# Decay exponents in a gated delta-rule layer: from a TensorE product to broadcast row sums with a per-partition bias

## Time and profile before

| | us |
|---|---|
| median of 3 runs | 4610.79 (4610.07 to 4611.10) |
| span of the profiled execution | 4601.9 |
| the median less that span | 8.9 |

### The profile page before, as it was taken

The page is one execution under the profiler, slowest core; times in us unless marked ns, Lnnn a source line. Parts: engine busy times, 40 slices in busy tenths (PEclk is TensorE's granted clock), DMA queues, the critical chain, the costliest instruction groups (busy, mean ns, idle before and its releaser), DMA issues. The chain is left out here.

```text
span 4601.9 us, 94001 instructions
## 1 busy us (share of the span) xinstructions
PE 4346.1 (94%) x31188; PEld 3239.7 (70%) x31188; DVE 3834.6 (83%) x8326; ACT 2846.0 (62%) x5356; POOL 2695.4 (59%) x8592
## 2 busy tenths in 40 slices
PE   4799999999999999999999999999999999998798
PEld 2477777777777777777777777777777777776444
DVE  6688988889888898888988889888888888985554
ACT  3466666666666666666666666666666666664111
POOL 1566666666666666666666666666666666664000
PEclk7899999999999999999999999999999999999899
DMA  3212212122121221212121221222222122120200
GB/s 106 45 41 48 49 35 48 41 48 50 34 59 39 50 48 34 50 48 50 36 58 42 47 48 39 45 50 48 48 47 46 42 47 49 38 44 20 70 14 19
DMA packets 575837, 209.77 MB, mean 46 GB/s; under 512 B 455180, under 2 KB 539660, under 8 KB 574328
## 3 DMA queue, kind: packets, MB, share of 16 engines
q1 hardware_dynamic: 574392, 200.48, 19.4%
q0 software_dynamic: 960, 3.28, 0.3%
HBM read 155.84 MB, written 47.81 MB: 44 GB/s over the span
## 5 line engine op out<-in xcount | busy, mean ns | idle before, releaser
L740 DVE SCALAR_TENSOR_TENSOR CV<-pp,CW,CV 128x1023 f32<-128x1023 f32 (+2 forms) x768 | 980.5, 1277 | 41.4 <-ACT CV L1122 24.5
L343 PE MATMUL pp<-A,W 128*128 128x512 f32 x2048 | 963.7, 599 | 14.9 <-DVE CV L740 9.3
L1414 POOL TENSOR_TENSOR UL<-UL,TM 128x126 f32<-128x126 f32 (+22 forms) x1984 | 735.1, 370 | 155.4
L1411 POOL TENSOR_TENSOR TM<-UL,XL 128x126 f32<-128x126 f32 (+22 forms) x1984 | 706.4, 356 | 148.3 <-issue 13.6
L343 PEld LDWEIGHTS pp<-A,W 128*128 128x128 f32 x2048 | 373.5, 193 | 312.8 <-issue 293.3
L1210 ACT ACTIVATE QE<-qa,TAB 128x128 f32<-128x128 f32 x1024 | 318.3, 362 | 425.6 <-PE qa L482 425.5
L863 DVE SCALAR_TENSOR_TENSOR St<-St,TAB,kv 128x128 f32<-128x128 f32 x1024 | 308.7, 343 | 234.9 <-PE kv L501 227.1
L1221 ACT ACTIVATE VS<-qa,EB 128x128 f32<-128x128 f32 x1024 | 319.2, 364 | 292.0 <-PE qa L492 286.0
L545 PE MATMUL emit<-Wo,NTr 128*128 128x256 f32 x2048 | 487.5, 381 | 1.1 <-ACT NTr L1255 1.1
L524 PE MATMUL emit<-Wz,A 128*128 128x256 f32 x2048 | 484.9, 380 | 1.6 <-DVE A L914 1.6
L900 DVE SCALAR_TENSOR_TENSOR CO<-CO,ty,SZ 128x128 f32<-128x128 f32 x1024 | 420.4, 469 | 64.3 <-POOL ty L1398 60.6
(11 more groups left out here) (232 smaller groups left out, 9463.4 us busy)
## 6 DMA issues: line engine op xcount, KB each, us to landing
W<-wqkv SPq DMA_DIRECT2D x256, 128.0 KB, 3.7
XL<-xb SPq DMA_DIRECT2D x128, 256.0 KB, 4.1
UL<-c_u SPq DMA_DIRECT2D x64, 256.0 KB, 2.9
xb<-X SPq DMA_DIRECT2D x512, 32.0 KB, 1.6
Wz<-wz SPq DMA_DIRECT2D x64, 256.0 KB, 2.7
ub<-UL SPq DMA_DIRECT2D x128, 128.0 KB, 2.9
N<-ub SPq DMA_DIRECT2D x256, 64.0 KB, 2.2
Wo<-wo SPq DMA_DIRECT2D x64, 256.0 KB, 3.8
```

The lines of the kernel that those rows point to most:

```text
L343: ins = t.matmul(bk.pp[:, 512 * h:512 * h + 512], m.W[:, c, k, :], m.xnT[:, w // KH % 2, c, 512 * h:512 * h + 512], start=c == 0, stop=c == 1)
L740: v.scalar_tensor_tensor(m.CV[:, t, d:S], bk.pp[:, 0:S - d], m.CW[:, w % KH, t, 3 - d:4 - d], m.CV[:, t, d:S], ALU.mult, ALU.add).then_inc ...
L1411: gp.tensor_tensor(m.TM[:, 0:a, 0:b], m.UL[:, 0:a, k:k + 1].to_broadcast([128, a, b]), m.XL[:, k, k + 1:32].unsqueeze(1).to_broadcast([128 ...
L1414: gp.tensor_tensor(m.UL[:, 0:a, k + 1:32], m.UL[:, 0:a, k + 1:32], m.TM[:, 0:a, 0:b], ALU.subtract).then_inc(s["sub"], 1)
```

## The change

Row sums stay in f32. The first one (gc, as rows) is written whole to DRAM, and one transfer per unit broadcasts the unit's two rows of 1024 values to all 128 partitions of a new tile GB (1 MB per unit, two buffers). The mask (0 or -1e30) is added to GB: on GpSimd (`gm`, two instructions of 128 x 1024 per unit), for units 0 and 1 on VectorE (`gmd`). The second row sum, as columns (AB), is the per-partition bias of the exponential: `dec` is now four ACTIVATEs of 128 x 128 for each quarter, sixteen per unit, in place in GB. `decp` and `mk` are gone, with GL, GR, DEC and the bf16 pieces. All four `dec` of a unit stand in ACT's order on both sides of `qe` of chunk 3, before `sz`. Each of `x` and `att` reads GB in place of DEC.

```diff
 SP
     def ldg(w):
-        sp.wait_ge(s["decp"], 4 * w)
-        for r in range(2):
-            q.dma_start(m.GR[3 * r:3 * r + 3, r, :], dr.gcd[2 * kh + r, :, t0:t0 + S]).then_inc(s["dg"], 16)
-        q.dma_start(m.GL[6:12], dr.gad[2 * kh:2 * kh + 2, :, t0:t0 + S]...).then_inc(s["dg"], 16)
+        sp.wait_ge(s["g3a"], 16)
+        if w > 1:
+            sp.wait_ge(s["strip"], STRIP["kq", w - 2, 3] + 1)
+        q.dma_start(m.GB[w % 2][:].rearrange("p r c t -> p r (c t)"),
+                    dr.gcd[32 * b + 2 * kh:32 * b + 2 * kh + 2, :].unsqueeze(0).to_broadcast([128, 2, S])).then_inc(s["dg"], 16)
+        if w:
+            sp.wait_ge(s["tabw"], 80)
+            sp.wait_ge(s["dec"], 4 * (w - 1))
+            q.dma_start(m.AB[w % 2][:], dr.abd[kh, :, b * CH:(b + 1) * CH, :]).then_inc(s["dg"], 16)
 start:
-        for k, d in enumerate((dr.gcd, dr.gad)):
-            sp.wait_ge(s["pieces"], 5 * k + 5)
-            q.dma_start(d[:, :, 0:S], p.pieces[k][0:32]).then_inc(s["g3a"], 16)
+        sp.wait_ge(s["gst"], 5)
+        q.dma_start(dr.gcd, p.ra).then_inc(s["g3a"], 16)
+        ldg(0)
 before the loop:
         xl(0)
+        ldg(1)
         ldw(1, 2)
 loop:
             decoded(u + 1)
-            ldg(u + 2)
+            ldg(u + 3)
             uo(u + 1)
 PE loop: the four decp(u + 2, q) are gone; pj(0, 2, h) moves from before the barrier to behind it
             qs(u, 5)
-            decp(u + 2, 0)
             pj(u + 2, 2, 0)
...
             sup(u, 5)
-            decp(u + 2, 1)
             at(u, 5)
...
             pj(u + 2, 2, 1)
-            decp(u + 2, 2)
             vn(u, 6)
...
             z(u, 2)
-            decp(u + 2, 3)
             m1(u + 1)
 DVE
-        v.tensor_tensor(m.DEC[n % 2][:], by(bk.strip[:], 4), g.mask..., ALU.min).then_inc(s["strip"], 1)
+    def gmd(w, r):
+        dv.wait_ge(s["dg"], 16 + 32 * w)
+        v.tensor_tensor(m.GB[w % 2][:, r], m.GB[w % 2][:, r], g.mask..., ALU.add).then_inc(s["gmd"], 1)
 DVE start: the ten instructions that make the pieces are gone; kred(0) moves behind the barrier
 DVE tables:
         dv.wait_ge(s["col"], 4)
+        v.tensor_copy(m.AB[0][:], p.BT[:, 0:CH, 0:2]).then_inc(s["ab"], 1)
+        for r in range(2):
+            gmd(0, r)
+        v.tensor_copy(tab(p, ROWJ), cols(p.BT)).then_inc(s["dtab"], 1)
 DVE loop: mk(u + 1, 0) to mk(u + 1, 3) are gone; gmd(1, 0) and gmd(1, 1) stand before the loop
 ACT
     def dec(w, q):
-        ac.wait_ge(s["strip"], STRIP["dec", w, q] + 1)
-        a.activation(m.DEC[n % 2][:], m.DEC[n % 2][:], ACT.Exp).then_inc(s["dec"], 1)
+        if w < 2:
+            ac.wait_ge(s["gmd"], 2 * w + 2)
+        else:
+            ac.wait_ge(s["gm"], 2 * (w - 1))
+        for c in range(2):
+            for r in range(2):
+                row = m.GB[w % 2][:, r, 2 * q + c, :]
+                ins = a.activation(row, row, ACT.Exp, bias=m.AB[w % 2][:, 2 * q + c, r:r + 1])
+        ins.then_inc(s["dec"], 1)
 ACT tables: dec(0, 0) to dec(0, 3) stand before the exponential of EGLB
 ACT loop:
             vs(u - 1, 2)
             vne(u - 1, 2)
+            dec(u + 1, 0)
+            dec(u + 1, 1)
             qe(u - 1, 3)
+            dec(u + 1, 2)
+            dec(u + 1, 3)
             sz(u - 1, 0)
             qt(u + 1)
             vs(u - 1, 3)
...
             qe(u - 1, 5)
-            dec(u + 1, 0)
             vs(u - 1, 5)
...
             sz(u - 1, 1)
-            dec(u + 1, 1)
             qe(u - 1, 6)
...
             vne(u - 1, 6)
-            dec(u + 1, 2)
             sz(u - 1, 2)
...
             nt(u - 1, 2)
-            dec(u + 1, 3)
             sq(u - 1, 3)
 POOL
+    def gm(w, r):
+        po.wait_ge(s["dg"], 16 + 32 * w)
+        gp.tensor_tensor(m.GB[w % 2][:, r], m.GB[w % 2][:, r], g.mask..., ALU.add).then_inc(s["gm"], 1)
 POOL start: the six gp.dma_start of the pieces are gone, nk(0) moves behind the barrier; tables writes a fifth table (abd)
 POOL loop:
             vsc(u + 1, 0)
+            gm(u + 3, 0)
+            gm(u + 3, 1)
             tv(u, 2)
```

More of the change, by code:

```diff
@@ L28 @@
 MAGIC = 1597463007.0
-EG, NEG, EGLB, EGLS = range(4)
+EG, NEG, EGLB, EGLS, ROWJ = range(5)
 SUB = 62
@@ L297, in loop @@
         nl(0)
+        ldg(2)
         ui(1)
@@ L374, in tpq @@
         ins.then_inc(s["tpq"], 1)
[L376 to L384, removed]
     def kq(w, q):
@@ L606, in loop @@
         tables()
-        decp(0, 0)
+        pj(0, 2, 0)
+        pj(0, 2, 1)
         kq(0, 0)
-        decp(0, 1)
         kq(0, 1)
-        decp(0, 2)
         kq(0, 2)
-        decp(0, 3)
         kq(0, 3)
@@ L1309, in tables @@
                          ACT.Exp).then_inc(s["egt"], 1)
+        for i in range(4):
+            dec(0, i)
         a.activation(tab(p, EGLB), cols(p.DL), ACT.Exp).then_inc(s["egt"], 1)
@@ L1431, in ng @@
                         ALU.mult).then_inc(s["EB"], 1)
+    def gm(w, r):
+        if not inside(w):
+            return
+        po.wait_ge(s["dg"], 16 + 32 * w)
+        gp.tensor_tensor(m.GB[w % 2][:, r], m.GB[w % 2][:, r], g.mask.unsqueeze(1).to_broadcast([128, CH, 128]),
+                        ALU.add).then_inc(s["gm"], 1)
     def vsc(w, h):
@@ L1477, in start @@
         gp.memset(m.N1[1][:], 0.0)
-        nk(0)
-        for k, d in enumerate((dr.gcd, dr.gad)):
-            po.wait_ge(s["pieces"], 5 * k + 5)
-            for b in range(1, NB):
-                gp.dma_start(d[:, :, b * S:b * S + S], p.pieces[k][32 * b:32 * b + 32]).then_inc(s["g3w"], 16)
     def tables():
         po.wait_ge(s["egt"], 4)
-        po.wait_ge(s["dtab"], 1)
+        po.wait_ge(s["dtab"], 2)
         for k in range(4):
@@ L1802, in program @@
 def program(nc, x, wqkv, wz, wo, convw, wba, dtb, alog, normw, lut, widx,
-            c_f32, c_mask, c_gr, c_reset, c_u0, out):
+            c_f32, c_mask, c_reset, c_u0, out):
     with ExitStack() as ctx:
@@ L1848, in program @@
             m.V = [alloc(lp, f"V{i}", [128, CH, 2, 128]) for i in range(2)]
-            m.DEC = [alloc(lp, f"DEC{i}", [128, 4, 128]) for i in range(2)]
+            m.GB = [alloc(lp, f"GB{i}", [128, 2, CH, 128]) for i in range(2)]
+            m.AB = [alloc(lp, f"AB{i}", [128, CH, 2]) for i in range(2)]
             m.X = [alloc(lp, f"X{i}", [128, 2 * CH, 128]) for i in range(2)]
@@ L1887, in program @@
             p.ra, p.rb, p.rc, p.rd = (m.QK[:, i, :] for i in (1, 2, 4, 5))
-            p.pieces = [m.X[1][:].rearrange("p u d -> p (u d)"), m.V[1][:].rearrange("p c r d -> p (c r d)")]
-            p.pieces = [t[:, 0:1536].bitcast(BF16).rearrange("p (k t) -> p k t", k=3) for t in p.pieces]
             p.GC, p.BT = (m.K[i][:].rearrange("p c (t h) -> p (c t) h", h=32) for i in (1, 2))
@@ L1940, in consts @@
     f[:, 128] = 1.0
[L1941 to L1943 removed]
+    mask = np.where(j > q, -1e30, 0.0).astype(np.float32)
     u0 = np.zeros((2, 64, 16, 32), np.float32)
```

129 lines of the change are left out of this document (42 added, 87 removed), and 2 rows, old and new, of the table SEMS.

## The result

The changed kernel takes 5080.62 us (median of 4 runs, 5065.87 to 5095.99); the kernel before 4610.94 in the same session (4610.07 to 4615.53). The ratio is 1.1024, 95% interval 1.1007 to 1.1041: 10% slower, where 0.6% was forecast. The range ended at 4725, so the result lies outside it.

The account below looks back on a forecast made before the run. PE was taken to set the pace; stall 1.92 less gain 1.27 gave +0.65 a turn, +40 us over 62 turns, less 12 at the start, plus 8.9 carried to the timed median: 4639 us, range 4565 to 4725.

Parts of the forecast that it names:

- What bounds the kernel: Steady turn of 64.03 us: PE, busy 62.55, sets the pace; other engines' delays cost only once PE must wait.
- What is hidden: POOL's two mask adds, 3.75 us together with 1.89 each, fit its idle 3.69 us before tv 2.
- if that cover were gone: If POOL's idle time did not cover the adds, nrm 2 on DVE would be late by the rest.
- The stall at `sup` 3: ACT's block of table loads and exponentials (0.26 us each) makes PE wait 1.92 us a turn at sup 3.
- still covered: DVE's state 3 starts near 2134.3 instead of 2134.1, before PE reaches ks 4 near 2135.2: no wait.
- Rival C: The stall at sup 3 lowers the granted clock, 1.4 us of slowness a turn: 4726 us; chance 0.06.
- The forecast without holds: Whole kernel with the adds hidden and the exponentials in one block: a turn of 64.7 us, 4639 us.
- PE's gain of 1.27: Second half of the turn: without decp and mk, PE gains 1.27 us a turn, bounds 0.9 and 1.9.
- Start: Work before the barrier goes, PE starts 16 us earlier; after costs, net 12 us gained, bounds 3 and 20.
- rival B: ACT's exponentials don't overlap, 0.362 us each: stall 3.5, net +2.25 a turn, 4738 us; chance 0.09.
- rival A: ACT's block (under about 4.8 us) is hidden, only PE's shorter list counts: 4520 us; chance 0.08.

Follow-up runs that it names:

- gm_dve: The changed kernel with the mask adds of all units on VectorE in front of nrm 0, none on GpSimd, exponentials still in one block; 4764.26 us.
- early_two_vsc_late: Changed kernel, mask adds on VectorE behind nrm 3, exponentials in two blocks (behind vne 2 and sz 1), GpSimd's first vsc moved behind nk; 4543.94 us.
- before_vsc_late: The kernel before, with only GpSimd's first vsc moved from behind on 1 to behind nk, in front of the second vsc; 4565.02 us.
- both: The changed kernel with GpSimd's mask adds issued after the second vsc and the exponentials in four groups at the old places; 4684.27 us.

## Why the prediction was wrong

- **What bounds the kernel.** Right: PE sets the pace, and a delay elsewhere costs one for one from the moment at which PE asks.
- **"What is hidden: the adds only take `vsc`'s place as `nrm` 1's neighbour."** This step failed, and with it 6.1 of the 7.1 us a turn that were missed (4.41 at `ctp` 1 and 1.66 behind it). I read the 1.96 of the earlier trace rows as a mild slowing and asked only whether POOL had 3.75 us free. It nearly had (3.69); the adds took 4.73, one 2.39 and not the 1.89 of `vsc`, which is not the same form (it takes one value per row where the adds take the mask), and that 1 us is in the hold too. The earlier trace rows held more: 0.83 us over the free 1.13 is one instruction of 1.17 us, which began when `vsc` had 1.02 to go and ended 0.15 behind it. Beside three GpSimd instructions in a row each of the first three is held. A cover of idle time on the engine that gets the work says nothing about the engine next to it. The prediction's words for "if that cover were gone" named `nrm` 2, the wrong victim.
- **The stall at `sup` 3.** Predicted 1.92, measured 2.34. The mechanism was right; the term mis-sized was the exponential: 0.26 taken from `qe`, 0.295 measured (eight in 2.36 us to the next start). The Trainium skill's figure (ScalarE: Activation LUTs, What ACT_TABLE_LOAD costs), an estimate of 0.29 us and a stall of 2.4, agrees with the trace. Its drain of 1.38 us doesn't show, and here the measurement decides: the exponentials begin 1.29 after the load does, and that is the load's own 1.28.
- **`state` behind the block "still covered".** Right: `ks` 4 starts directly behind `ctp` 0 at 2063.16, without a wait. But PE now waits for St 0.5 us a turn at `ks` 6, where the trace of before has nearly nothing. `decp` 1 and the 0.17 us that it waited for `att` stood in front of that `ks`; without them PE asks 0.39 us sooner, and `state` 5 starts 0.19 later behind its `sup` than before (0.83 for 0.64 us). So part of what the shorter list gives is lost there.
- **Rival C.** The slow clock came, behind the 5 us wait. The stall at `sup` 3 alone can do the same. In gm_dve, with that stall in every turn and no hold by adds, the way from `sup` 3 to the next `vn` takes 5.3 to 5.4 us in 28 turns and 6.8 to 7.0 in 32; in the changed kernel it is slow in 2 of 58. Two such stretches of gm_dve, in the order of the earlier trace rows (the clock is the third number from the end):

```profile
2145.07:2150.42 5.35, 5.34 (x34) 4.88 (x35) 5.32 (x11) 4.04 (x8) 4.51 (x11) 1.00 0.00 0
2211.32:2218.31 6.99, 6.99 (x34) 6.34 (x35) 6.80 (x12) 4.14 (x8) 5.37 (x15) 0.76 0.01 2
```

  That is 0.9 us a turn (32 of 60 turns at 1.65), so C, at 0.06, was a part of the truth for the kernel with the adds hidden. What decides which turns are slow stays open.
- **The forecast without holds.** gm_dve measured 4764 for 4639. Of the 125 us, 18.6 lie at the start, as told above. Its turn is 66.3 us, where 64.7 was forecast: 1.6 a turn. The terms that I find are 0.42 at `sup` 3, 0.54 at `ks` and 0.9 of slow matmuls, 1.9 in all; against them stands a wait of `decp` for `att` that went with it (13.7 us in all before), 0.2 a turn. Even with the failed step mended I should have been 2.6% low, from the same habit of taking each cover as whole.
- **PE's gain of 1.27.** In the steady turns it hardly reaches the end. early_two_vsc_late and before_vsc_late have the same turn within 0.05 us, though PE's list is 1.1 us shorter in the first; 0.6 of the 1.27 was `mk` 1 in front of `ctp` 1, and that wait is gone in both. The wait for St takes back about half of the 1.1 (36.2 us in all). How the rest divides between ScalarE's four table loads and the adds on VectorE (2.35 us) was not measured.
- **Start.** Predicted `x` of quarter 3 at 105.5; measured 106.65 (119.10 before). PE's first transposes behind the barrier start at 64.44, near 67 predicted, and `pj` waits for W once, 4.4 us. The state is first cleared at 169.6 us, 9.4 earlier than before, for a net 12 predicted. The steps held. The broadcast landed in 4.9 us where 7.7 was taken, and no wait of GpSimd between 300 and 4500 us names a transfer.
- **Two slips of arithmetic.** The net of rival B is 3.5 - 1.27 = 2.23 a turn, not 2.25, and rival A's block of 4.8 us needs exponentials of 0.14 (4.8 less two loads, over 16), not 0.12. Neither moves the forecast.

## What to carry to other kernels

Idle time on GpSimd isn't free to fill: list what VectorE executes beside it, and if that has two operands in SBUF, or is a lookup of the `lm` kind, price it at the full length of the longest GpSimd instruction. A row of four instructions whose mean is 1.7 times that of its equals elsewhere is a hold that is already there, and moving its neighbour may be the cheapest gain in the kernel (here 0.9% by one line). When two costs share a place, take both away before judging either. And before a difference of two times is divided by the number of turns, look where it lies: here 21 us looked like 0.34 a turn and were mostly gained before the first one.

## What the runs showed of the hardware

- A VectorE instruction with both tensor inputs in SBUF that starts beside a running GpSimd instruction lasts until about 0.15 us behind its end (in each of the four cases followed in the kernels before and after), so up to the length of one: 2430 ns beside 2387, 1886 beside 1893, free 337. The same for `lm`, a TENSOR_SCALAR with its tensor input and output in SBUF: 2406 ns in the kernel both, whose adds last up to 2429, and 337 free. `x` and `att`, with one input in PSUM, are never longer than 487 ns in any of these kernels, adds or not.
- The Trainium skill (SBUF — State Buffer, Who interferes with whom) says that a VectorE instruction with two SBUF inputs contends with a GpSimd instruction that reads SBUF, and calls the shared ports an exclusive lock: whoever issues first has them for the whole instruction (said there of VectorE's 2-port modes), and the other is blocked. These traces agree, down to `x`, which it exempts; that GpSimd is blocked where VectorE starts first isn't looked at here. By that rule and the prediction's own 1.89 us for each of `vsc` and the two adds, the estimate for `nrm` 1 would have been 3 x 1.89 + 0.34 = 6.0 us; the trace has 6.79, with adds of 2.39. The page was not drawn on in the prediction.
- TensorE comes back slow after a wait of 4.8 to 5 us (1.12 for 0.60 us in `ctp`, 3.12 to 3.62 for 1.88 in `pj`; granted clock 0.56 over 3.87 us), and in 32 of 60 turns of gm_dve after one of 2.34 (granted clock 0.76 over 6.99 us, 1.00 in the turns that stay fast).
- Cutting the GpSimd instruction limits the hold and doesn't remove it: `nrm` 1 beside sixteen short adds takes 1.96 us and beside four pieces of `vsc` 2.27, where it is 1.13 free.
